# Attention with q's angles as pairs of 32-row products, v's sum taken from x's sum, and a new order on VectorE and GpSimd

## The chip, the cores and the metric

The kernel runs on one core of a Trainium2 chip. The metric is the device time of the whole launch in microseconds (us); smaller is better. The core has TensorE (PE: matmuls; PEld is its weight load), VectorE (DVE), ScalarE (ACT), GpSimd (POOL) and SyncE (SP, which here only issues DMAs). TensorE, VectorE, ScalarE and GpSimd each take their instructions in the order in which they are written; they meet through semaphores.

## What is computed

A layer of attention and a layer of experts over 8 sequences of 512 tokens with 128 features. Cut to what matters here, the attention is:

```python
q = (x @ Wq.T + bq).reshape(B, 512, 16, 8)      # k and v alike; 16 heads of 8
def fourier(h):
    p = einsum('blhd,dm->blhm', h, proj_mat) / sqrt(8)     # 128 angles a head
    return concatenate([cos(p), sin(p)], -1) / sqrt(128)
kv  = einsum('blhm,blhd->bhmd', fourier(k), v)
out = einsum('blhm,bhmd->blhd', fourier(q), kv)
x   = layernorm(x + out.reshape(B, 512, 128) @ Wo.T + bo)
# then: router, top 2 of 8 experts, two matmuls an expert, a second layernorm
```

Sine and cosine of p are made from p in turns: p/(2 pi), less its nearest whole number, and then sin(2 pi r) and the square of sin(pi r), since cos(2 pi r) = 1 - 2 sin(pi r)^2.

## The kernel before

**Stages.** A start-up of some 14 us, the attention over 8 sequences (`sequences(body)`, called batches 0 to 7 here), each of 16 units of work, and then the experts: 71 tiles of 128 rows, of which the last batch's layernorm, router and ranks are carried along. The end sums and normalizes.

**A unit** is 1024 columns of angles on 128 partitions: units 0 to 7 are k's, units 8 to 15 are q's. In unit u TensorE issues, in this order, `angles` of u (two 128x512 products into one of three PSUM slots of `ang`), `reduce_turns` of u-1 (minus the identity times the rounded turns, added to the same slot), and then one product with finished features: `kv_product` in units 4 to 11, `out_product(b, hg, a)` from unit 13 on and in units 0 to 3 of the next batch. Around them stand the pieces of a batch that come once: `x_T`, `project` (units 6 and 7, for batch b+1), `rows_T` (unit 8), `logits` (unit 9), `kv_turn` and `ranks` (unit 12), `c_product` (unit 14), `v_product` (unit 15). `rows_T`, `logits` and `ranks` belong to batch b-1.

**Angles.** q and k are each split in two float32r parts, written to `parts_dram` and read back by DMA as `stk`, 128 rows for 4 heads: 4 combinations of parts times 8 dimensions times 4 heads. `proj_stk` holds the projection for these rows, zero outside a head's own 32 rows. Before the change these 32 rows are spread over all partitions (dimension outside, head inside), so that each of q's products runs over all 128 rows.

**VectorE** rounds a unit's turns (`round_turns`, L1073), squares its share of the units two behind (`square`, L1081), and takes values out of PSUM: `kvT_evac`, `kv_evac`, `c_evac`, `v_evac`, `x_evac`, `take_logits`, `largest`, `which`, `take_ranks`, `move_base`, `slot_numbers`. The tuples BEFORE_ROUND, AFTER_ROUND and AFTER_SQUARE say at which unit and where in it they stand.

**ScalarE** runs the two sines of a unit (L885, L886) when the unit is reduced.

**GpSimd** squares the units of `POOL_SQ` (L1450), and for batch b-1 normalizes (`deviation`, `normalize`, L1475), picks experts (`chosen`; L1600 writes `picks`, for which `ranks` waits), and sends the rows with 8 indirect DMAs (`send_rows`, L1619) in units 14 and 15; for batch b+1 it splits k and q (L360).

**kv.** `kv_product` sums the features times v; `kvT_evac` takes both halves to SBUF, `kv_turn` turns them with two matmuls and adds -2 times v's sum with four more (L626), `kv_evac` copies the result to `kv_pad`, for which the first `out_product` waits. `c_product` makes the constant that `out_evac` adds.

## Time and profile before

| | before |
|---|---|
| time, median of 3 runs | 527.19 us (527.05 to 529.71) |
| the profiled execution: time, span of its instructions | 527.94 us, 526.1 us |
| granted TensorE clock, mean of the span | 0.976 |
| busy: PE, PEld, DVE, ACT, POOL | 484.8, 289.3, 411.4, 371.3, 393.2 us |
| batches 1 to 6 of the attention, each | 41.0 us |
| batch 0, from its first angles to batch 1's | 39.0 us |
| DMA moved | 53.94 MB, mean 103 GB/s |

The span runs from the profile's first instruction to the end of its last, 1.8 us less than the device time of that execution. "Busy" is the time in which an engine has an instruction of its own under way; matmuls overlap, so the distance from one group's start to the next one's start says more of TensorE than the sum of durations. A number in square brackets in a row is idle time of the engine ahead of the instruction, with what ended it.

### The profile page before, as it was taken

The page shows a single profiled execution, that of the slowest core. Times are in us where ns is not written, and L with a number is a line of the kernel's source. Part 1 is how long each engine was busy: PE and PEld are TensorE (multiplying, and loading weights), DVE is VectorE, ACT ScalarE, POOL GpSimd, SP SyncE. Part 2 cuts the span into 40 slices and gives each one's busy share as a digit, 9 for nine tenths or more (in the row PEclk, how much of TensorE's full clock was granted, in tenths as well). Part 3 has the DMA queues.
Part 4 walks back from the last instruction along what each step waited for, and adds up shares of the span by engine and source line. Part 5 has one row for each costly group of instructions (what it writes and reads, how often), then busy time and mean ns, then how long its engine had stood idle before and what let it go on. Part 6 is the DMA issues. An engine that isn't in the chain of part 4 may idle for free.

```text
span 526.1 us, 12307 instructions
## 1 busy us (share of the span) xinstructions
PE 484.8 (92%) x3819; PEld 289.3 (55%) x3819; DVE 411.4 (78%) x897; ACT 371.3 (71%) x505; POOL 393.2 (75%) x463
## 2 busy tenths in 40 slices
PE   6699999999999999999999999878999999999813
PEld 3344344345345345345334444438999988999801
DVE  4878978979979888888888887567678976777554
ACT  3698797887898798788788786576555555565225
POOL 2374298888888889779779879985777787687645
PEclk9899999999999999999999999899999999999957
DMA  4563053144154143244233221032222333222184
GB/s 110 168 198 122 21 161 121 52 132 154 47 161 159 40 143 126 65 127 150 67 110 122 87 61 46 2 73 59 72 62 73 88 97 101 68 73 63 37 307 177
DMA packets 44596, 53.94 MB, mean 103 GB/s; under 512 B 8419, under 2 KB 25093, under 8 KB 44533
## 3 DMA queue, kind: packets, MB, share of 16 engines
q1 hardware_dynamic: 39728, 43.82, 28.1%
q0 software_dynamic: 4320, 8.95, 5.2%
q8 instruction: 33, 0.54, 0.4%
q10 hardware_dynamic: 484, 0.38, 0.2%
q14 instruction: 31, 0.25, 0.1%
HBM read 33.09 MB, written 20.04 MB: 101 GB/s over the span
## 4 chain that ended last, share of the span: by engine, by line
PE 67%; POOL 15%; DMA 4%; issue 4%; SPq 3%; DVE 3%; ACT 2%; DVEq 0%; POOLq 0%; ACTq 0%
PE misc L647 11%; PE ang L798 10%; PE ang L807 10%; PE ang L592 8%; PE misc L612 6%; PE ang L584 6%; POOL rows_s L1475 5%; PE ang L579 5%; POOL feats L1450 4%; PE misc L531 1%; POOL rstd L1468 1%; ACT feats L886 1%; PE misc L678 1%; PE misc L626 1%; PE misc L662 1%
## 5 line engine op out<-in xcount | busy, mean ns | idle before, releaser
L1073 DVE TENSOR_SCALAR turns<-ang 128x1024 f16<-128x1024 f32 x128 | 155.9, 1219 | 48.8 <-PE ang L584 29.7
L885 ACT ACTIVATE feats<-ang 128x1024 f32<-128x1024 f32 x128 | 131.3, 1026 | 63.1 <-PE ang L592 62.2
L1450 POOL TENSOR_TENSOR feats<-feats 128x1024 f32<-128x1024 f32 x56 | 107.8, 1925 | 58.8 <-ACT feats L886 58.4
L886 ACT ACTIVATE feats<-ang 128x1024 f32<-128x1024 f32 x128 | 131.1, 1024 | 0.0
L1081 DVE TENSOR_TENSOR feats<-feats 128x1024 f32<-128x1024 f32 x72 | 93.2, 1295 | 0.9 <-ACT feats L886 0.9
L1619 POOL DMA_INDIRECT routed_dram<-rows_s,slots x64 | 76.5, 1195 | 19.2 <-issue 18.2
L1649 POOL DMA_INDIRECT expert_dram<-feats x71 | 69.8, 983 | 25.8 <-DVE feats L1374 16.9
L592 PE MATMUL ang<-turns,negi 128*128 128x512 f16 x256 | 77.9, 386 | 4.0 <-DVE turns L1073 4.0
L798 PE MATMUL ang<-feats 128*128 128x128 f32 x568 | 76.5, 278 | 3.2 <-ACT feats L953 1.4
L953 ACT ACTIVATE feats<-experts 128x644 f32 x71 | 52.5, 739 | 34.9 <-DVE feats L1374 27.5
L807 PE MATMUL ang<-experts,feats 128*128 x568 | 75.6, 276 | 0.5 <-DVE feats L1334 0.5
L798 PEld LDWEIGHTS ang<-feats 128*128 128x128 f32 x568 | 68.9, 192 | 6.8 <-DVE feats L1326 3.7
L612 PE MATMUL misc<-feats,v_pad 128*32 128x256 f32 x1024 | 70.0, 393 | 2.4 <-POOL feats L1450 2.4
L807 PEld LDWEIGHTS ang<-experts,feats 128*128 128x128 f32 x568 | 69.1, 192 | 1.3 <-issue 1.3
L647 PE MATMUL misc<-feats,kv_pad 128*32 128x512 f32 x512 | 66.1, 602 | 0.0
L1334 DVE TENSOR_TENSOR feats<-ang,feats 128x512 f32<-128x512 f32 x71 | 48.9, 689 | 21.4 <-PE ang L798 21.2
L612 PEld LDWEIGHTS misc<-feats,v_pad 128*32 128x32 f32 x1024 | 27.2, 110 | 41.7 <-issue 27.5
L579 PE MATMUL ang<-proj_stk,stk 128*128 128x512 f32 x128 | 48.8, 464 | 1.2 <-DMA stk<-parts_dram 0.6
L584 PE MATMUL ang<-stk,proj_stk 128*128 128x512 f32 x128 | 49.1, 465 | 0.0
L970 ACT ACTIVATE feats<-feats 128x128 f32<-128x128 f32 x71 | 28.1, 396 | 17.7 <-DVE feats L1383 8.5
L592 PEld LDWEIGHTS ang<-turns,negi 128*128 128x128 f16 x256 | 14.9, 99 | 41.7 <-issue 28.8
L579 PEld LDWEIGHTS ang<-proj_stk,stk 128*128 128x128 f32 x128 | 20.0, 191 | 32.2 <-issue 30.9
(201 smaller groups left out, 570.1 us busy)
## 6 DMA issues: line engine op xcount, KB each, us to landing
stk<-parts_dram SPq DMA_DIRECT2D x126, 128.0 KB, 2.7
parts_dram<-parts SPq DMA_DIRECT2D x16, 512.0 KB, 3.3
feats<-routed_dram SPq DMA_DIRECT2D x72, 65.5 KB
experts<-ffn_W SPq DMA_DIRECT2D x16, 256.0 KB, 3.2
feats<-expert_dram SPq DMA_DIRECT2D x16, 256.0 KB, 4.8
out<-feats SPq DMA_DIRECT2D x8, 256.0 KB, 2.0
x_all<-attn_x SPq DMA_DIRECT2D x7, 256.0 KB, 4.5
expert_dram<-feats POOLq DMA_INDIRECT x71
```

The lines of the kernel that those rows point to most:

```text
L579: mm = pe.matmul(a[:, t * 512:(t + 1) * 512], stk[:, 0, hg, tok:tok + P], proj_stk[:, :, :].rearrange("p g m -> p (g m)"), start=True, sto ...
L584: mm = pe.matmul(a[:, t * 512:(t + 1) * 512], proj_stk[:, 2 * half + t, :], stk[:, 1, hg, :], start=True, stop=False, skip_group_check=True)
L592: mm = pe.matmul(ang[:, slot(ph, u), t * 512:(t + 1) * 512], negi[:, :], turns[:, u % 2, t * 512:(t + 1) * 512], start=False, stop=True, s ...
L612: mm = pe.matmul(misc[32 * g:32 * g + 32, 0, 0:2 * FEAT].rearrange("p (a m) -> p a m", a=2), v_pad[:, 2 * half + t, g, hg * PADH:(hg + 1) ...
L647: mm = pe.matmul(misc[32 * g:32 * g + 32, 1, :], kv_pad[:, a, g, hg * PADH:(hg + 1) * PADH], feats[:, 2 * hg + g // 2, a, (g % 2) * LEN:(g ...
L798: mm = pe.matmul(h_bank[r % 2][:, j * P:(j + 1) * P], w_now[:, r % W_RING, j * P:(j + 1) * P], xgT[:, r % 2, :], start=True, stop=True)
L807: mm = pe.matmul(y_bank[r % 2][:, 0:P], hidT[:, r % 2, j * P:(j + 1) * P], expert(x_e)[:, j * P:(j + 1) * P], start=(j == 0), stop=(j == H ...
L885: act.activation(f[:, 0, :], a, ACT.Sin, scale=TWO_PI)
L886: act.activation(f[:, 1, :], a, ACT.Sin, scale=TWO_PI / 2).then_inc(s["sines"], 1)
L1073: dve.tensor_scalar(turns[:, u % 2, :], ang[:, slot(ph, u), :], MAGIC, -MAGIC, ALU.add, ALU.add)\
L1081: dve.tensor_tensor(f, f, f, ALU.mult).then_inc(s["sq_v"], 1)
L1450: pool.tensor_tensor(f, f, f, ALU.mult).then_inc(s["sq_p"], 1)
```

## The change

- **q's angles.** The operand is ordered by head: in `parts_dram` and `stk` a head's 32 rows (2 parts of the projection, 2 parts of q, 8 dimensions) stand together. q's product of head g takes only rows 32g to 32g+31, and the two heads of a unit stand on different rows of the array and write different banks. k's products are as before. Both copies are now made by the write: four DMAs of 256 KB where one of 512 KB stood; a read is one DMA of 256 KB where two of 128 KB stood. The projection's setup has one DMA instead of four and one more step on VectorE.
- **The reduction** of units 8 to 14 is cut into 32-column pieces: 8 matmuls with 8 weight loads instead of 2 with 2.
- **v's sum.** `x_evac` also sums x over the tokens, `v_total` (unit 9) makes v's sum with one small product, and `kvT_evac` adds it (times -2) while it copies; the four matmuls of L626, the scaled identity, `c_product` and the copy to `kv_c` go, and `kv_turn` is two transposes. `c_evac` now sums kvT itself, in two instructions.
- **Order on VectorE.** In unit 11 the square of unit 9 no longer stands behind `kvT_evac`; it stands in unit 12, behind `kv_evac`, `take_ranks` and `move_base`, which all come ahead of it.
- **Order on GpSimd.** It also squares unit 14, in unit 0 of the next batch, and of its 8 indirect DMAs two go out in each of units 14, 15, 0 and 1.

```diff
-POOL_SQ = (1, 3, 4, 6, 8, 10, 12)
+POOL_SQ = (1, 3, 4, 6, 8, 10, 12, 14)
...
                 hold(sp, "split", 2, b, side + 1)
-                dst = parts_dram[b, side].rearrange("i r n -> r i n")
-                sp.dma_start(dst, parts[:, side, :, :].bitcast(F32)).then_inc(s["parts_out"], 16)
-                hold(sp, "parts_out", 32, b, 16 * side + 16)
+                for j in range(PARTS):
+                    for i in range(PARTS):
+                        sp.dma_start(parts_dram[b, side, :, j, i], parts[:, side, i, :].bitcast(F32))\
+                            .then_inc(s["parts_out"], 16)
+                hold(sp, "parts_out", 32 * SPL, b, 16 * SPL * (side + 1))
...
                     for t in range(2):
-                        mm = pe.matmul(a[:, t * 512:(t + 1) * 512], proj_stk[:, 2 * half + t, :],
-                                       stk[:, 1, hg, :], start=True, stop=False, skip_group_check=True)
+                        g = 2 * half + t
+                        rows = slice(g * PADH, (g + 1) * PADH)
+                        mm = pe.matmul(a[:, t * 512:(t + 1) * 512], proj_stk[rows, g, :], stk[rows, 1, hg, :],
+                                       start=True, stop=False, skip_group_check=True)
...
+                tiles = [slice(32 * i, 32 * i + 32) for i in range(G)] if HALF <= u < UNITS - 1 else [slice(0, P)]
                 for t in range(2):
-                    mm = pe.matmul(ang[:, slot(ph, u), t * 512:(t + 1) * 512], negi[:, :],
-                                   turns[:, u % 2, t * 512:(t + 1) * 512], start=False, stop=True,
-                                   skip_group_check=True)
+                    for cols in tiles:
+                        mm = pe.matmul(ang[cols, slot(ph, u), t * 512:(t + 1) * 512], negi[:, cols],
+                                       turns[:, u % 2, t * 512:(t + 1) * 512], start=False, stop=True,
+                                       skip_group_check=True)
...
+            def v_total(b, *free):
+
+                wait(pe, *free)
+                pe.matmul(misc[:, 1, P:P + 2], wT[:, 2, :], x_sum[:, b % 2, :], start=True, stop=True,
+                          skip_group_check=True).then_inc(s["v_sum_mm"], 1)
...
                 wait(pe, "kvT_ev", 1, b, 1)
-                o = misc[:, 0, :]
-                pe.matmul(o[:, 0:P], kvT[:, 0, :], ident[:, :], start=True, stop=True, skip_group_check=True)
-                pe.matmul(o[:, P:2 * P], kvT[:, 1, :], ident4[:, :], start=True, stop=False, skip_group_check=True)
-                for t in range(LT):
-                    mm = pe.matmul(o[:, P:2 * P], minus_2[:, :], dense(v_pad[:, t, :, :]),
-                                   start=False, stop=(t == LT - 1), skip_group_check=True)
+                for a in range(2):
+                    mm = pe.transpose(misc[:, 0, a * P:(a + 1) * P], kvT[:, a, :], ident[:, :])
                 mm.then_inc(s["kv_mm"], 1)
...
             def kvT_evac(b):
                 wait(dve, "kvT_mm", HALF, b, HALF)
-                dve.tensor_copy(kvT[:, :, :].rearrange("p a m -> p (a m)"), misc[:, 0, 0:2 * P])\
-                    .then_inc(s["kvT_ev"], 1)
+                wait(dve, "v_sum_ok", 1, b, 1)
+                dve.tensor_scalar(kvT[:, 1, :], misc[:, 0, FEAT:2 * FEAT], 4.0, v_sum[:, :], ALU.mult, ALU.add)
+                dve.tensor_copy(kvT[:, 0, :], misc[:, 0, 0:FEAT]).then_inc(s["kvT_ev"], 1)
...
             def c_evac(b):
-                wait(dve, "c_mm", 1, b, 1)
+                wait(dve, "kvT_ev", 1, b, 1)
+                dve.tensor_reduce(c_raw[:, :], kvT[:, 1, :], AX.X, ALU.add).then_inc(s["c_raw_ok"], 1)
+                wait(dve, "c_raw_ok", 1, b, 1)
...
                     if u == 11:
                         kvT_evac(b)
+                    if u == 12:
+                        kv_evac(b)
...
-                    if not (first and u < 2):
+                    if not (first and u < 2) and u != 11:
                         square(b, u - 2)
+                    if u == 12:
+                        square(b, 9)
...
                     if u in (14, 15) and not first:
-                        send_rows(b - 1, u - 14)
+                        send_rows(b - 1, 0, range(2 * (u - 14), 2 * (u - 13)))
+                    if u in (0, 1) and b > 1:
+                        send_rows(b - 2, 1, range(2 * u, 2 * u + 2))
```

VectorE in units 11 to 14 of a batch, before (L1073 rounds a unit, L1081 squares one, L1085 is `kvT_evac`, L1147 `take_ranks`, L1092 and L1093 `kv_evac`, L1152 `move_base`, L1158 `slot_numbers`):

```order
L1073 TENSOR_SCALAR turns<-ang 128x1024
L1085 COPY kvT<-misc 128x256
L1081 TENSOR_TENSOR feats<-feats 128x1024
L1073 TENSOR_SCALAR turns<-ang 128x1024
L1147 TENSOR_TENSOR slot_m<-misc,base 128x32
L1092 COPY kv_c<-misc 128x128
L1093 COPY kv_pad<-misc 128x32x8
L1152 TENSOR_TENSOR base<-misc,base 128x8
L1073 TENSOR_SCALAR turns<-ang 128x1024
L1081 TENSOR_TENSOR feats<-feats 128x1024
L1158 TENSOR_REDUCE slots<-slot_k 128x8
L1073 TENSOR_SCALAR turns<-ang 128x1024
```

And in the changed kernel (L1079 rounds, L1087 squares, L1098 and L1099 are `kvT_evac`, L1105 `kv_evac`, L1161 `take_ranks`, L1166 `move_base`):

```order
L1079 TENSOR_SCALAR turns<-ang 128x1024
L1098 TENSOR_SCALAR kvT<-misc,v_sum 128x128
L1099 COPY kvT<-misc 128x128
L1079 TENSOR_SCALAR turns<-ang 128x1024
L1105 COPY kv_pad<-misc 128x32x8
L1161 TENSOR_TENSOR slot_m<-misc,base 128x32
L1166 TENSOR_TENSOR base<-misc,base 128x8
L1087 TENSOR_TENSOR feats<-feats 128x1024
L1079 TENSOR_SCALAR turns<-ang 128x1024
L1087 TENSOR_TENSOR feats<-feats 128x1024
L1172 TENSOR_REDUCE slots<-slot_k 128x8
L1079 TENSOR_SCALAR turns<-ang 128x1024
```

The first square, unit 9's, has moved from ahead of the rounding of unit 12 to behind all that unit 12 takes out of PSUM.

GpSimd from the picks of unit 11 to unit 3 of the next batch, before (L1600 writes `picks`, L1450 squares, L1611 is `slots_of_picks`, L1619 sends):

```order
L1600 TENSOR_TENSOR picks<-hot 128x32
L1602 TENSOR_TENSOR rows_s<-top 128x4
L1603 COPY rows_s<-pick_no 128x4
L1604 TENSOR_SCALAR rows_s<-rows_s 128x4
L1450 TENSOR_TENSOR feats<-feats 128x1024
L1611 TENSOR_TENSOR slot_k<-hot,slot_m 128x32 x2
L1450 TENSOR_TENSOR feats<-feats 128x1024
L1619 DMA routed_dram<-rows_s,slots 38016x131 x8
L1450 TENSOR_TENSOR feats<-feats 128x1024 x3
```

And in the changed kernel (L1620, L1468, L1631, L1639):

```order
L1620 TENSOR_TENSOR picks<-hot 128x32
L1622 TENSOR_TENSOR rows_s<-top 128x4
L1623 COPY rows_s<-pick_no 128x4
L1624 TENSOR_SCALAR rows_s<-rows_s 128x4
L1468 TENSOR_TENSOR feats<-feats 128x1024
L1631 TENSOR_TENSOR slot_k<-hot,slot_m 128x32 x2
L1468 TENSOR_TENSOR feats<-feats 128x1024
L1639 DMA routed_dram<-rows_s,slots 38016x131 x4
L1468 TENSOR_TENSOR feats<-feats 128x1024
L1639 DMA routed_dram<-rows_s,slots 38016x131 x4
L1468 TENSOR_TENSOR feats<-feats 128x1024 x3
```

The square of unit 14 now stands between the first and the second four of the eight sends; the rest of the row is as it was.

## Rows read from the trace of the kernel before

**Rows 1.** One steady stretch: start:end, us, each engine's busy time (instructions), granted clock, DMA

```profile
139.00:180.00 41.00, 40.74 (x320) 17.90 (x315) 35.34 (x57) 34.21 (x40) 34.69 (x33) 1.00 0.39 117
```

**Rows 2.** Waits of TensorE from 56 to 346 us: total us, times, longest

```profile
PE misc L671 <- POOL rows_s L1475: 1.8, 7, 0.3
```

**Rows 3.** The chain within 150 to 200 us, in order: start us, us, what

```profile
150.09 1.90 POOL feats L1450
...
157.34 0.66 PE misc L671 x4
...
161.92 1.00 PE misc L612 x16
```

**Rows 4.** Timeline of TensorE, four single matmuls of unit 10: start us, us

```profile
160.76 0.48 PE L584 MATMUL ang<-stk,proj_stk 128*128 128x512 f32 x1
...
161.08 0.40 PE L584 MATMUL ang<-stk,proj_stk 128*128 128x512 f32 x1
...
161.32 0.39 PE L592 MATMUL ang<-turns,negi 128*128 128x512 f16 x1
...
161.54 0.38 PE L592 MATMUL ang<-turns,negi 128*128 128x512 f16 x1
```

**Rows 5.** Timeline of TensorE, units 12 to 15 and unit 0's start

```profile
166.43 1.06 PE L626 MATMUL misc<-v_pad,minus 128*128 128x128 f32 x8
167.32 0.18 PE L688 MATMUL misc<-picks,tri 128*128 128x32 f16 x1
...
170.50 0.74 PE L584 MATMUL ang<-stk,proj_stk 128*128 128x512 f32 x2
...
173.29 0.60 PE L592 MATMUL ang<-turns,negi 128*128 128x512 f16 x2
...
175.74 0.70 PE L579 MATMUL ang<-proj_stk,stk 128*128 128x512 f32 x2
```

**Rows 6.** Timeline of VectorE in the same batch: squares (L1081) and a rounding (L1073)

```profile
159.65 1.82 DVE L1081 TENSOR_TENSOR feats<-feats 128x1024 f32<-128x1024 f32 x1
...
165.44 1.22 DVE L1081 TENSOR_TENSOR feats<-feats 128x1024 f32<-128x1024 f32 x1
...
169.55 1.21 DVE L1081 TENSOR_TENSOR feats<-feats 128x1024 f32<-128x1024 f32 x1
...
171.27 1.22 DVE L1073 TENSOR_SCALAR turns<-ang 128x1024 f16<-128x1024 f32 x1 [0.38 <-PE ang L584]
```

**Rows 7.** Timeline of GpSimd in the same batch, and its picks in the experts' stage

```profile
158.49 1.89 POOL L1450 TENSOR_TENSOR feats<-feats 128x1024 f32<-128x1024 f32 x1
160.34 2.26 POOL L360 TENSOR_TENSOR parts<-qk_f,parts 128x512 fp32r<-128x512 f32 x1
...
165.68 1.09 POOL L1600 TENSOR_TENSOR picks<-hot 128x32 f16<-128x32 f32 x1
...
167.24 1.89 POOL L1450 TENSOR_TENSOR feats<-feats 128x1024 f32<-128x1024 f32 x1
...
388.36 0.25 POOL L1600 TENSOR_TENSOR picks<-hot 128x32 f16<-128x32 f32 x1
```

**Rows 8.** Timeline of ScalarE: the two sines of unit 11

```profile
166.19 1.02 ACT L885 ACTIVATE feats<-ang 128x1024 f32<-128x1024 f32 x1 [0.17 <-PE ang L592]
167.11 1.02 ACT L886 ACTIVATE feats<-ang 128x1024 f32<-128x1024 f32 x1
```

**Rows 9.** Timeline of GpSimd at the attention's end: the fourth of the eight sends

```profile
349.58 1.52 POOL L1619 DMA_INDIRECT routed_dram<-rows_s,slots  x1 [0.30 <-issue]
```

**Rows 10.** Timeline of TensorE there: last four out_products, first layer of the first tile

```profile
350.63 1.92 PE L647 MATMUL misc<-feats,kv_pad 128*32 128x512 f32 x16
352.49 1.16 PE L798 MATMUL ang<-feats 128*128 128x128 f32 x8
```

**Rows 11.** Timeline of TensorE in batch 7: a wait and the group behind it

```profile
330.36 1.93 PE L612 MATMUL misc<-feats,v_pad 128*32 128x256 f32 x16 [2.38 <-POOL feats L1450]
```

**Rows 12.** Timeline of TensorE at the start, unit 2's angles

```profile
17.46 0.74 PE L579 MATMUL ang<-proj_stk,stk 128*128 128x512 f32 x2 [0.63 <-DMA stk<-parts_dram]
```

More of the change, by code:

```diff
@@ L384, in write @@
                 hold(sp, "split", 2, b, side + 1)
[L385 to L387 removed]
+                for j in range(PARTS):
[3 more added lines that the diff above has]
+                hold(sp, "parts_out", 32 * SPL, b, 16 * SPL * (side + 1))
             def read(b, side, hg):
                 hold(sp, "angles", UNITS, b, HALF * side + 2 * hg + 2 - UNITS)
[L393 to L397 removed]
+                rows = parts_dram[b, side].rearrange("(a g) j i d n -> a (g j i d) n", a=HG)
+                sp.dma_start(stk[:, side, hg, :].bitcast(F32), rows[hg]).then_inc(stk_in[side][hg], 16)
             def at_unit(b, u):
@@ L569, in angles @@
                 elif u == 0:
-                    wait(pe, stk_in[0][0], 16 * PARTS, b, 0)
+                    wait(pe, stk_in[0][0], 16, b, 0)
                 elif half == 0:
-                    wait(pe, stk_in[side][hg], 16 * PARTS, b, 16 * PARTS)
+                    wait(pe, stk_in[side][hg], 16, b, 16)
                 wait(pe, "sines", UNITS, b, u - RING + 1)
@@ L756, in body @@
                         rows_T(b - 1, *(("b2_ok", 1, 0, 2) if last else ("q_ev", 1, b, 2)))
-                    if u == 9 and not first:
-                        logits(b - 1, "xr_ev", 1, b, 0)
+                    if u == 9:
+                        v_total(b, *(("q_ev", 1, b, 2) if first else ("xr_ev", 1, b, 0)))
+                        if not first:
+                            logits(b - 1, "xr_ev", 1, b, 0)
                     if u == 12:
@@ L766, in body @@
                     if u == 14:
-                        c_product(b)
                         out_product(b, 1, 0)
@@ L868, in proj_evac @@
                 wait(act, "split", 2, b, side - 1)
-                wait(act, "parts_out", 32, b, 16 * side - 16)
+                wait(act, "parts_out", 32 * SPL, b, 16 * SPL * (side - 1))
                 act.activation(parts[:, side, 0, :], misc[:, bank, :], ACT.Identity,
@@ L913, in _ @@
             act.dma_start(negi[:, :], c_negi).then_inc(s["negi_in"], 16)
+            for g in range(G):
+                act.dma_start(bv_col[g * PADH:(g + 1) * PADH, :],
+                              bv.rearrange("(a g d) -> g a d", a=HG, g=G)[g].unsqueeze(2)).then_inc(s["bv_in"], 16)
             act.dma_start(b1_raw[:, :], b1.rearrange("e (j p) -> (e j) p", p=P)).then_inc(s["b1_in"], 16)
-            act.wait_ge(s["consts"], 1)
+            act.wait_ge(s["consts"], 2)
             act.activation(warm[:, :], zero_t[:, :], ACT.Sin)
@@ L1268, in _ @@
             LAST_ROUND = ((7, bias_add), (8, bias_add))
-            BEFORE_ROUND = ((6, moments), (10, take_logits), (13, move_base))
-            AFTER_ROUND = ((5, residual), (10, largest))
-            AFTER_SQUARE = ((5, statistics), (10, which), (12, take_ranks), (13, slot_numbers))
+            BEFORE_ROUND = ((6, moments), (10, take_logits))
+            AFTER_ROUND = ((5, residual), (10, largest), (12, take_ranks), (12, move_base))
+            AFTER_SQUARE = ((5, statistics), (10, which), (13, slot_numbers))
             def body(b, ph):
```

101 lines of the change are left out of this document (50 added, 51 removed).

## The prediction

> **What bounds the kernel now.** I read the windows first. In a steady stretch of 41 us TensorE has 40.74 us of work at the full granted clock; the others have 34 to 35 us [rows 1]. Six of the eight batches are such stretches. But the work is in a ring. TensorE's waits name GpSimd's normalize seven times, 0.3 us at the longest [rows 2], and the chain of waits goes through GpSimd from the square of unit 4 (150.09) over normalize to `rows_T` at 157.34 [rows 3], 7.25 us of GpSimd's own work that TensorE's units 5 to 7 just cover. The second such place is `picks`: GpSimd writes them from 165.68 to 166.77 [rows 7], and `ranks` starts at 167.32 [rows 5], 0.5 us behind. What TensorE saves ahead of `ranks` beyond that is waited away, unless picks come sooner.
>
> **One rule of the two engines, from rows.** VectorE's square of 159.65 takes 1.82 us where others take 1.21 [rows 6]; GpSimd's square of 158.49 is under way until 160.4 [rows 7]. 159.65 + 1.82 - 1.21 = 160.26: it began 1.77 us behind the start of GpSimd's square. GpSimd's split of 160.34 then takes 2.26 us and begins in effect when VectorE's square is over. And the picks take 1.09 us beside the square of 165.44, but 0.25 us in the experts' stage, where there is none [rows 6, 7]. So: VectorE's square and GpSimd's tensor_tensor exclude each other, and whoever comes second waits for the whole instruction. The Trainium skill says the same (SBUF — State Buffer, the section on the shared port: an exclusive lock, held for the whole instruction, also for a tensor_tensor with both inputs in SBUF); by that rule, the trace agrees, and the collisions below follow from the new order.
>
> **The parts on TensorE.** Single starts: 160.76, 161.08, 161.32, 161.54 [rows 4]. A float32r product of 512 columns takes 0.24 us, a float16 one 0.22, and the first of the angles 0.32, of which some 0.10 is its weights' load. The 16 matmuls of `kv_product` stand four side by side: 4 x 0.22 = 0.87 us; in the chain they take 1.00 [rows 3], so 0.13 goes to the change between 128-wide and 32-wide work (0.10) and a load. A bare unit is 0.10 + 0.10 + 0.48 + 0.44 + 0.13 + 0.87 = 2.12 us.
> - Two products on 32 rows each: if they run side by side, as the 32-column ones do, the angles cost 0.24 instead of 0.48; if not, 0.48 (nothing gained). No row shows row pieces; I take 0.24, since the column pieces do run together.
> - The reduction in 32-column pieces: two rounds of 0.22 as before, and the change of shape now stands ahead of it rather than behind it. A bare unit: 2.12 - 0.24 = 1.88. Where whole-array work is a neighbour (units 8, 9, 10, 12, 13), seven more changes a batch come in at 0.10: 0.7 us.
> - `kv_turn`: L626 is 167.32 - 166.43 = 0.89 us [rows 5], gone; the two transposes instead of four passes save 0.2; `c_product` 0.1; `v_total` adds 0.2.
> - Sum a batch: 8 x 0.24 - 0.7 + 0.89 + 0.2 + 0.1 - 0.2 = 2.2 us (0.3 without the side-by-side). If TensorE alone bounded: 8 x 2.2 = 17.6 us.
> The Trainium skill says (TensorEngine Tiling (Array Packing), Key Properties) that a change of tiling mode drains the engine, and the trace agrees with 0.10 for it. The Trainium skill also gives, in TensorE: Matmul & The Clock Gate (Part 3), 3.07x for four row tiles, which no row here shows; by it the 0.24 stands.
>
> **What becomes of it: one batch, step by step**, in times of the trace before, with the same start of the chain (GpSimd's square of unit 4 at 150.09).
> 1. To `rows_T` nothing changes. From there TensorE saves some 0.2 us up to unit 11 and 1.1 in unit 12, so it is at `ranks` at about 166.0 instead of 167.3.
> 2. Picks: unit 9's square is no longer beside them, so they take 0.25: ready at 165.93 instead of 166.77. Both arrive together. Unit 13's angles start at 166.2 instead of 167.5: 1.3 us gained.
> 3. GpSimd goes on to its square of unit 10 at 166.40 (167.24 before [rows 7]). VectorE comes to unit 9's square at 166.9, since `take_ranks` must follow `ranks` (picks + 0.7 at the earliest), and GpSimd's square follows the picks by 0.47. So VectorE always comes second: 166.40 + 1.77 = 168.17, done 169.3.
> 4. TensorE does angles (166.2 + 0.45), reduction (to 167.2) and out_product(0, 0) (to 168.1) and then waits 1.25 us for unit 9's square. It ends unit 13 at 170.2; before 170.5 [rows 5]. Of the 1.3 us 0.3 is left.
> 5. VectorE rounds unit 13 until 170.43 and wants unit 11's square. GpSimd, behind its slots (169.24 + 0.45), starts unit 12's square at 169.69; the sines it needs end at 169.5 (two sines, 0.92 apart, take 1.84 us a unit [rows 8], and unit 12's follow unit 11's at 167.64). So the square waits until 169.69 + 1.77 = 171.46, before 169.55 [rows 6]. The rounding of unit 14, which stands behind it, runs 172.7 to 173.94; before it began at 171.27 and even waited for TensorE [rows 6].
> 6. TensorE wants to reduce unit 14 at 172.6, gets to at 174.0 (173.29 before [rows 5]), and with 0.46 + 0.87 + 0.1 + 0.92 begins the next batch at 176.35; before 175.74 [rows 5]. 0.6 us lost.
> 7. In units 0 to 5 VectorE has one square less, worth 0.14 us of a wait in unit 4. GpSimd's square 14 and later sends end near 187.4, ahead of the use of unit 1's square. Its later start of unit 4's square is 0.47 us, which closes the ring: a batch is 41.0 + 0.47 = 41.5 us.
>
> **The other terms.** Batch 0 has no ranks but both collisions: +0.35 (-2 without them). Batches 1 to 6: 6 x 0.47 = 2.8. Batch 7: its GpSimd carries the tables of the experts, which bind at the same times as before: 0. At its end GpSimd's fourth send ends at 351.1 [rows 9]; then comes unit 14's square, 1.89 us, until 353.0, and the last out_product, which before started at 351.55 (350.63 + 0.92) and let the first tile start at 352.49 [rows 10], waits for it: +1.5. The start: unit 2's angles waited for the read of `stk` at 17.46 [rows 12]; the write is now four DMAs and twice the bytes, 1 to 2 us later, of which 1 is hidden behind VectorE's setup; Wv's load comes about 0.6 sooner: 0, between -0.6 and +1. In the steady batches reads come ten units ahead of use; nothing. Sum: 527.94 + 0.35 + 2.8 + 1.5 = 532.6 for the profiled execution; the median lies 0.75 below that execution, so 531.8, taken as 532.0. A difference under 0.5% is about what cannot be told from none.
>
> **Rivals.**
> - *Only the first collision* (20%). Point 5 hangs on 0.74 us: if unit 12's sines come behind 170.43, VectorE goes first, its square is done at 171.6, unit 14 is reduced at 173.0, and the batch is 40.5: 6 x -0.5 - 0.5 + 1.5 = -2.0, 525.2. Slower products on TensorE (no side-by-side: 0.9 us later at `ranks`) lead there.
> - *TensorE's gain is kept* (30%). For it: 2.2 us a batch are really taken out, GpSimd has 6 us without work in 41 [rows 1] and loses two waits, and squares may meet more kindly than in my walk. Against: steps 3 to 6. With some 1.7 us in each of seven batches and +1.5 at the end: 527.2 - 10.4 = 517; all of it, 2.2 x 7, gives 513.
> - *The clock falls in the new waits* (7%). After the wait of 2.38 us in batch 7 the next group takes 1.93 us instead of the usual 1.07 [rows 11], at 1.2 GHz. If the waits of steps 4 and 6 bring that once a batch, at about 1.7 us: 532 + 6 x 1.7 = 542, slower. It decides only if two waits of 1.3 us, 3 us apart, count like one long one.
> - *Both collisions* as forecast (43%), 529.5 to 534.5.
>
> **How the numbers follow.** Time 532.0. Faster by over 0.5% (below 524.6): the kept gain 0.30 and a third of the first rival, 0.07: 0.37. Within 0.5%: the rest of the first rival and the forecast's lower edge: 0.19. Slower: 0.44. The range of 8 in 10 goes from 515 to 537 and leaves out the full 2.2 us and the clock's fall; the forecast's own range is 529.5 to 534.5.
>
> **What would show it.** Steady batches 41.5 us apart; picks of 0.25 us; VectorE's square in unit 12 some 2.4 us long; idle TensorE of over 1 us ahead of the second out_product of unit 13 (released by a VectorE square) and ahead of unit 14's reduction (released by the rounding); bare q units of 1.88 us; the last out_product of batch 7 released by GpSimd's square. It is wrong if batches are 39 us apart, if the angles' pair starts 0.24 us or more apart, or if those waits are not there.

## The result, and the profile after

| | before | after |
|---|---|---|
| time, median of 4 runs each | 528.12 us (527.05 to 529.71) | 532.97 us (531.88 to 534.42) |
| the profiled execution: time, span | 527.94, 526.1 us | 531.88, 530.1 us |
| batch 1 begins (first angles) | 52.8 us | 52.2 us |
| a steady batch (2 to 6) | 41.00 us | 41.42 us |
| batch 7 begins | 298.7 us | 300.7 us |
| first layer of the first tile begins | 352.49 us | 356.22 us |
| from there to the end | 173.6 us | 173.8 us |

The ratio is 1.0091 (95% interval 1.0063 to 1.0120): the change makes the kernel 0.9% slower. TensorE has less work, and the kernel does not get shorter. The ratios of the experiments below leave out runs over 1.5% above the fastest of their own kernel: three of the ten of e3 (544.9 to 551.7 us) and two of the six of e7 (541.2 and 548.0 us), none of any other.

One steady batch of the changed kernel (the columns are those of [rows 1]):

```profile
134.90:176.38 41.48, 39.02 (x351) 15.90 (x349) 37.88 (x59) 33.95 (x39) 37.30 (x35) 1.00 0.49 141
```

TensorE had 40.74 us of work in 41.00 [rows 1] and now has 39.02 in 41.48; VectorE went from 35.34 to 37.88 us and GpSimd from 34.69 to 37.30. GpSimd has one square of 1.89 us more; VectorE has one of 1.21 us less and a few small steps more. The rest is time in which the two hold each other up, and it counts as busy. TensorE's waits from 56 to 300 us, which before were one line of GpSimd's [rows 2], are now:

```profile
PE ang L594 <- DVE turns L1079: 7.1, 6, 1.2
PE misc L645 <- DVE feats L1087: 6.5, 6, 1.1
PE misc L669 <- POOL rows_s L1493: 1.1, 6, 0.2
```

Two waits in each batch, 1.1 us for a square (L1087) and 1.2 us for a rounding (L1079). Here they are in the timeline of TensorE, batch 3, units 12 to 15:

```profile
166.12 0.19 PE L686 MATMUL misc<-picks,tri 128*128 128x32 f16 x1
...
167.40 1.07 PE L645 MATMUL misc<-feats,kv_pad 128*32 128x512 f32 x8
169.54 1.06 PE L645 MATMUL misc<-feats,kv_pad 128*32 128x512 f32 x8 [1.08 <-DVE feats L1087]
...
174.06 0.62 PE L594 MATMUL ang<-turns,negi 128*32 128x512 f16 x8 [1.19 <-DVE turns L1079]
...
176.38 0.71 PE L577 MATMUL ang<-proj_stk,stk 128*128 128x512 f32 x2
```

VectorE at the same place (L1087 squares units 9 and 11, L1079 rounds units 13 and 14):

```profile
167.17 2.32 DVE L1087 TENSOR_TENSOR feats<-feats 128x1024 f32<-128x1024 f32 x1
169.41 1.21 DVE L1079 TENSOR_SCALAR turns<-ang 128x1024 f16<-128x1024 f32 x1
170.55 2.20 DVE L1087 TENSOR_TENSOR feats<-feats 128x1024 f32<-128x1024 f32 x1
...
172.79 1.21 DVE L1079 TENSOR_SCALAR turns<-ang 128x1024 f16<-128x1024 f32 x1
```

And GpSimd (picks, squares of units 10 and 12, the first send):

```profile
165.81 0.25 POOL L1620 TENSOR_TENSOR picks<-hot 128x32 f16<-128x32 f32 x1
...
166.52 1.89 POOL L1468 TENSOR_TENSOR feats<-feats 128x1024 f32<-128x1024 f32 x1
168.37 1.44 POOL L1631 TENSOR_TENSOR slot_k<-hot,slot_m 128x32 f32<-128x32 f32 x2
169.77 1.89 POOL L1468 TENSOR_TENSOR feats<-feats 128x1024 f32<-128x1024 f32 x1
173.16 1.13 POOL L1639 DMA_INDIRECT routed_dram<-rows_s,slots  x1 [1.50 <-DVE slots L1172]
```

Both of VectorE's squares begin while one of GpSimd's is under way, 0.65 and 0.78 us behind its start, and they take 1.1 and 1.0 us longer than the 1.21 of [rows 6]. Each ends 1.08 us behind the end of GpSimd's, whenever it began. VectorE has three more such squares in a steady batch of the changed kernel (of units 15, 2 and 7: 1.42, 2.63 and 1.85 us), and the kernel before has two (1.47 and 1.82 us); TensorE waits for none of these. The roundings, which read PSUM, are not held: 1.19 to 1.23 us beside GpSimd's squares, in all profiles.

At the hand-over to the experts, GpSimd's fourth send, its square of unit 14, and TensorE's last out_product and the first tile (compare [rows 9] and [rows 10]):

```profile
351.26 1.89 POOL L1639 DMA_INDIRECT routed_dram<-rows_s,slots  x1 [0.30 <-issue]
353.18 1.90 POOL L1468 TENSOR_TENSOR feats<-feats 128x1024 f32<-128x1024 f32 x1
```

```profile
355.23 1.06 PE L645 MATMUL misc<-feats,kv_pad 128*32 128x512 f32 x8 [2.19 <-POOL feats L1468]
356.22 1.16 PE L797 MATMUL ang<-feats 128*128 128x128 f32 x8
```

### The profile page after: what moved, and what is told of

The parts are those of the page before. It is cut to its first block, busy times and chain, and to the rows that moved or that the text cites. A ratio compares the mean times of both kernels' runs of the same rounds, so it can differ in the third digit from the quotient of the medians.

```text
span 530.1 us, 12861 instructions
## 1 busy us (share of the span) xinstructions
PE 469.9 (89%) x4075; PEld 272.1 (51%) x4075; DVE 430.1 (81%) x914; ACT 368.8 (70%) x505; POOL 411.0 (78%) x471
## 4 chain that ended last, share of the span: by engine, by line
PE 46%; POOL 22%; DVE 15%; issue 9%; DMA 4%; SPq 3%; ACT 2%; ACTq 0%; DVEq 0%; POOLq 0%
PE ang L797 10%; PE ang L806 10%; POOL feats L1468 7%; DVE turns L1079 6%; PE misc L645 6%; POOL rows_s L1493 5%; PE ang L577 5%; PE ang L594 5%; DVE feats L1087 5%; PE misc L614 3%; POOL routed_dram L1639 2%; POOL rstd L1486 1%; PE misc L529 1%; PE misc L660 1%; ACT feats L885 1%
## 5 line engine op out<-in xcount | busy, mean ns | idle before, releaser
L1079 DVE TENSOR_SCALAR turns<-ang 128x1024 f16<-128x1024 f32 x128 | 155.6, 1217 | 36.6 <-PE ang L577 19.2
L1468 POOL TENSOR_TENSOR feats<-feats 128x1024 f32<-128x1024 f32 x64 | 126.4, 1975 | 38.9 <-ACT feats L885 37.3
L1087 DVE TENSOR_TENSOR feats<-feats 128x1024 f32<-128x1024 f32 x64 | 107.3, 1677 | 2.3 <-ACT feats L885 2.3
L1639 POOL DMA_INDIRECT routed_dram<-rows_s,slots x64 | 75.1, 1173 | 26.0 <-issue 15.9
L594 PE MATMUL ang<-turns,negi 128*32 128x512 f16 (+1 forms) x592 | 79.6, 390 | 11.2 <-DVE turns L1079 11.2
L645 PE MATMUL misc<-feats,kv_pad 128*32 128x512 f32 x512 | 68.6, 610 | 10.5 <-DVE feats L1087 8.3
L614 PE MATMUL misc<-feats,v_pad 128*32 128x256 f32 x1024 | 68.4, 387 | 2.2 <-POOL feats L1468 2.2
L614 PEld LDWEIGHTS misc<-feats,v_pad 128*32 128x32 f32 x1024 | 28.6, 110 | 36.8 <-issue 20.5
L594 PEld LDWEIGHTS ang<-turns,negi 128*32 128x32 f16 (+1 forms) x592 | 15.1, 95 | 47.2 <-DVE turns L1079 26.5
L1392 DVE SCALAR_TENSOR_TENSOR feats<-ang,feats 128x128 f32<-128x128 f32 x71 | 24.8, 349 | 10.8 <-PE ang L806 10.3
```

Of the source, the lines that this page charges most:

```text
L594: mm = pe.matmul(ang[cols, slot(ph, u), t * 512:(t + 1) * 512], negi[:, cols], turns[:, u % 2, t * 512:(t + 1) * 512], start=False, stop=True,
L614: mm = pe.matmul(misc[32 * g:32 * g + 32, 0, 0:2 * FEAT].rearrange("p (a m) -> p a m", a=2), v_pad[:, 2 * half + t, g, hg * PADH:(hg + 1) ...
L645: mm = pe.matmul(misc[32 * g:32 * g + 32, 1, :], kv_pad[:, a, g, hg * PADH:(hg + 1) * PADH], feats[:, 2 * hg + g // 2, a, (g % 2) * LEN:(g ...
L1079: dve.tensor_scalar(turns[:, u % 2, :], ang[:, slot(ph, u), :], MAGIC, -MAGIC, ALU.add, ALU.add)\
L1087: dve.tensor_tensor(f, f, f, ALU.mult).then_inc(s["sq_v"], 1)
L1468: pool.tensor_tensor(f, f, f, ALU.mult).then_inc(s["sq_p"], 1)
```

## The experiments

They ran on three other chips of the same kind (e1 to e4, e5 to e8, e9 to e12), on which the kernel before takes 542.7 to 543.7 us (medians of 23 to 29 runs). The steady batches repeat there unit by unit to 0.03 us; the experts' stage takes 12 to 15 us more. So each is compared with the kernel before on its own chip, and the mechanism is read from the lengths of the units: from the start of one unit's angles to the next one's, in a steady batch (2 to 6; the middle one of the five). In the table u9 is unit 9 and so on, and "bare" is a unit without any piece that comes once a batch (10 and 11). Unit 12 has `kv_turn` and `ranks`, unit 13 the first two out_products, unit 15 `v_product`.

```
                                u9    bare   u12   u13   u15   batch  ratio to before (95%)
before                         3.01   2.11   2.56  2.97  3.01  41.00  1
after (e5 repeats it)          3.05   1.84   1.62  4.14  4.01  41.42  1.0043 (1.0025-1.0060)
e1 square 9 early              3.05   1.84   2.32  3.31  2.75  41.17  1.0008 (0.9983-1.0034)
e2 square 14 on VectorE        3.05   1.84   1.62  4.14  4.01  41.54  1.0034 (1.0013-1.0055)
e3 both                        3.05   1.84   2.32  3.31  2.75  40.13  0.9888 (0.9852-0.9923)
e4 whole rows and reductions   3.23   2.11   1.44  3.79  4.46  42.10  1.0100 (1.0053-1.0147)
e6 before, with the new order  3.01   2.11   2.56  3.18  3.02  41.22  0.9972 (0.9948-0.9997)
e7 e3 and early writes         3.05   1.84   2.32  3.31  2.75  40.15  0.9864 (0.9813-0.9915)
e8 e3, whole reductions        3.18   1.97   2.27  3.31  2.88  40.75  one run
e9 e3, whole rows, reductions  3.23   2.11   1.44  4.16  3.02  41.20  1.0015 (0.9985-1.0045)
e10 square 11 late             3.05   1.84   1.62  4.14  3.41  40.85  0.9953 (0.9933-0.9973)
e11 e10, square 14, writes     3.05   1.84   1.62  4.14  3.41  40.94  0.9976 (0.9950-1.0002)
```

Theory A is the prediction's: VectorE's squares of units 9 and 11 come second behind GpSimd's of units 10 and 12, and that eats TensorE's gain. Theory B: GpSimd, with eight squares, is full.

**e1: square 9 early.**

```diff
-                    if not (first and u < 2) and u != 11:
+                    if not (first and u < 2):
                         square(b, u - 2)
-                    if u == 12:
-                        square(b, 9)
```

> The changed kernel, with unit 9's square back in unit 11, behind kvT_evac; all else as changed. Theory A (the two collisions of VectorE's squares 9 and 11 with GpSimd's squares 10 and 12 eat TensorE's gain): the picks take about 1.1 us again, but unit 13 no longer waits for a square, and VectorE is free for the square of unit 11 before GpSimd starts unit 12's; a steady batch falls from 41.42 to about 40.0 us (39.7 to 40.3), the whole to 522 us (520 to 525). Theory B (GpSimd, which now has eight squares, is full: in the changed kernel it works from 178.79 to 193.50 without a gap, and has 37.3 us of work and 2 us between its DMA issues in 41.4 us, so that the ring runs through it): the batch stays within 0.4 us of 41.42, the whole at 529 to 533.

Both waits of units 13 and 15 go, and batch 1 takes 39.97 us (41.34 in e5), as Theory A has it. But batches 2 to 6 take 41.17, outside the 39.7 to 40.3 expected: unit 2's reduction now waits 0.86 us. The timelines of VectorE, GpSimd and TensorE there:

```profile
177.50 2.54 DVE L1087 TENSOR_TENSOR feats<-feats 128x1024 f32<-128x1024 f32 x1
```

```profile
177.04 1.90 POOL L1466 TENSOR_TENSOR feats<-feats 128x1024 f32<-128x1024 f32 x1
```

```profile
181.84 0.61 PE L594 MATMUL ang<-turns,negi 128*128 128x512 f16 x2 [0.86 <-DVE turns L1079]
```

GpSimd's square of unit 14, sent ahead of VectorE's of unit 15 by 0.46 us, is a third collision. In batch 1 it isn't there: no sends stand before it (they begin with batch 1's own, in its unit 14). So the eighth square does cost, but by the moment at which it runs, not because GpSimd is full; Theory B has the number and not the mechanism.

**e2: square 14 on VectorE** (POOL_SQ without 14).

> The changed kernel, with unit 14's square back on VectorE. Theory A: the batch is set by the collisions of units 12 to 14, which stay; a steady batch stays at 41.4 us (41.2 to 41.6), and only the hand-over gains: the last out_product of batch 7 no longer waits for GpSimd (2.19 us of wait go), so the whole is 530 us (529 to 531). Theory B: GpSimd loses 1.89 us a batch; batches fall by over 1 us, the whole to 523 or less.

Batches of 41.54 us, as Theory A said, and B falls. The hand-over's wait for GpSimd is gone; what the last out_product then waits for is 0.28 and 0.72 us of data for the experts' transposes ahead of it. Alone, the edit gains nothing that shows clearly against e5.

**e3: both.**

> The changed kernel with both edits: unit 9's square in unit 11, unit 14's square on VectorE. Theory A: the gain of e1 and the hand-over's of e2 add up: 520 us (517 to 523), faster than the kernel before (528) too. Theory B: GpSimd relieved and the order restored, about 520 too; if B alone is right, e3 is as e2.

40.13 us a batch, 1.1% faster than the kernel before, and 1.3 us a batch under the changed kernel. Its ten runs spread more than those of the kernel before on this chip (534.9 to 551.7 us against 541.5 to 546.6); over all ten the median is 1.1% lower and the mean 0.6%. TensorE's waits from 51 to 293 us:

```profile
PE misc L686 <- POOL picks L1618: 3.7, 6, 0.6
PE ang L594 <- DVE turns L1079: 1.4, 6, 0.2
PE misc L669 <- POOL rows_s L1491: 1.1, 6, 0.2
```

The ring is back at `picks`, 0.6 us a batch, because square 9 stands beside them again, and the three waits of a batch sum to 1.0 us. The picks:

```profile
164.11 0.95 POOL L1618 TENSOR_TENSOR picks<-hot 128x32 f16<-128x32 f32 x1
```

**e4: whole rows and reductions** in the changed kernel.

```diff
-mm = pe.matmul(..., proj_stk[rows, g, :], stk[rows, 1, hg, :],
+mm = pe.matmul(..., proj_stk[:, g, :], stk[:, 1, hg, :],
...
-tiles = [slice(32 * i, 32 * i + 32) for i in range(G)] if HALF <= u < UNITS - 1 else [slice(0, P)]
+tiles = [slice(0, P)]
```

> The changed kernel, with q's products over all 128 rows of the array and the reduction of units 8 to 14 in whole products, as before; the operand order and all else as changed. TensorE then has 8 x 0.24 = 1.9 us a batch more of products and 0.7 less of changes of shape. Theory A: TensorE's time is waited away in units 13 and 14 anyway, but GpSimd's square of unit 12 comes later with its sines and VectorE's behind it; a batch is 41.4 to 42.1 us, the whole 532 to 537 us. Rival C (TensorE's gain does carry over into the time): 1.2 us a batch more, 541 us.

42.10, the upper end of Theory A. TensorE comes later to unit 13, the first collision shrinks (VectorE's square of unit 9 takes 1.64 us), the second grows (2.81 us), and the wait ahead of unit 14's reduction is 1.3 us. TensorE's 0.27 us a unit, 2.2 us a batch, are worth 0.68 us a batch while the collisions stand.

**e5: the changed kernel again**, on the chip of e6 to e8.

> The changed kernel itself, on the chip of the other runs of this group, to be set beside them. Its attention should repeat: steady batches of 41.42 us, batch 1 to start at 52.2 us, the last out_product of batch 7 waiting 2.2 us for GpSimd's square of unit 14. Its ratio to the kernel before was 1.009; the same here, 1.005 to 1.013, if the difference lies in the attention alone.

The steady batches repeat. Batch 1 begins at 53.6 us and not at 52.2, and the ratio is 1.0043, just under the range expected. Both are taken up with e12.

**e6: the kernel before with VectorE's new order only.**

```diff
-BEFORE_ROUND = ((6, moments), (10, take_logits), (13, move_base))
-AFTER_ROUND = ((5, residual), (10, largest))
-AFTER_SQUARE = ((5, statistics), (10, which), (12, take_ranks), (13, slot_numbers))
+BEFORE_ROUND = ((6, moments), (10, take_logits))
+AFTER_ROUND = ((5, residual), (10, largest), (12, take_ranks), (12, move_base))
+AFTER_SQUARE = ((5, statistics), (10, which), (13, slot_numbers))
...
+                    if u == 12:
+                        kv_evac(b)
...
-                    if not (first and u < 2):
+                    if not (first and u < 2) and u != 11:
                         square(b, u - 2)
+                    if u == 12:
+                        square(b, 9)
...
-                    if u == 12:
-                        kv_evac(b)
```

> The kernel before, with only VectorE's new order of units 11 to 13 (unit 9's square in unit 12, behind take_ranks, kv_evac and move_base); operand, reduction, v's sum, GpSimd's squares and sends as before. Theory A (the order brings the collisions): TensorE is at ranks at 167.3, so VectorE comes to unit 9's square at about 168.3 to 168.7, behind GpSimd's square of unit 10, which now starts at 166.4; the second out_product of unit 13 waits some 0.5 us, unit 11's square comes second behind GpSimd's square of unit 12, and unit 14's reduction waits over 1 us; steady batches of 41.7 to 42.3 us, the whole 1.0 to 1.8% slower than the kernel before. Rival D (the order costs only where TensorE has become faster): 40.8 to 41.2 us a batch, the same time as before.

41.22: below Theory A's range and at the upper end of its rival's. The order alone costs 0.22 us a batch, and the times show how near it is. VectorE, squares of units 9 and 11:

```profile
166.34 1.29 DVE L1081 TENSOR_TENSOR feats<-feats 128x1024 f32<-128x1024 f32 x1
...
168.69 1.21 DVE L1081 TENSOR_TENSOR feats<-feats 128x1024 f32<-128x1024 f32 x1
```

GpSimd, squares of units 10 and 12 and the slots between:

```profile
164.37 1.89 POOL L1452 TENSOR_TENSOR feats<-feats 128x1024 f32<-128x1024 f32 x1
166.30 1.44 POOL L1613 TENSOR_TENSOR slot_k<-hot,slot_m 128x32 f32<-128x32 f32 x2
168.72 2.94 POOL L1452 TENSOR_TENSOR feats<-feats 128x1024 f32<-128x1024 f32 x1 [0.97 <-ACT feats L886]
```

VectorE's square of unit 9 comes just as GpSimd's of unit 10 ends, and its square of unit 11 comes 0.03 us ahead of GpSimd's, which then takes 2.94 us, at nobody's cost. The same order that loses a lock twice in the changed kernel loses it hardly once here, since TensorE reaches `ranks` 1.3 us later.

**e7: e3 with early writes.** For batch 0 the high parts are written when ScalarE has made them, ahead of VectorE's split.

```diff
+                if first:
+                    sp.wait_ge(s["kq"[side] + "_ev"], 1)
...
+                for i in range(PARTS):
+                    if first and i:
+                        sp.wait_ge(s["split"], side + 1)
+                    for j in range(PARTS):
```

> The changed kernel with unit 9's square back in unit 11 and unit 14's square on VectorE, and at the start, for batch 0, the two writes of the high parts of k and q issued as soon as ScalarE has made them, ahead of VectorE's split, and those of the low parts behind it. Steady batches of 40.13 us. If unit 2's angles wait for the four issues of the write in a row (2.49 us, from 10.59), the wait of 3.5 us ahead of them falls by 1.2 us and batch 1 starts at 50.3 us instead of 51.5; if they wait for the transfers of twice the bytes, it stays within 0.3 us of 51.5. The whole: 1.1 to 1.5% faster than the kernel before.

Unit 2's angles wait 2.68 us instead of 3.56 for `stk`, and batch 1 starts at 50.4 instead of 51.5. So when the write is issued matters; that the four issues in a row are the cause is not shown. They still take 2.50 us (2.49 in e3) and only begin 0.75 us sooner, at 10.15, and the read is issued 5.35 us behind that, as in e3. In the kernel before one issue of 0.39 us stands there and the read follows 2.8 us behind it.

The batches are those of e3. The ratio is 1.4% under the kernel before; the six runs lie between 531.7 and 548.0 us, and their median is 0.7% under. So e3 and e7 can't be told apart. Its profiled execution shows one thing that may spread them: VectorE and ScalarE stand still in batch 6 with a releaser that the profile calls "remote" (the trace names no instruction for it), and the batch takes 44.75 us. On VectorE:

```profile
258.80 1.22 DVE L1085 TENSOR_SCALAR turns<-ang 128x1024 f16<-128x1024 f32 x1 [1.37 <-remote]
```

**e8: e3 with whole reductions.**

> The changed kernel with unit 9's square in unit 11 and unit 14's on VectorE, and the reduction of units 8 to 14 in whole products instead of 32-column pieces. By the prediction's price of a change of shape, 0.10 us, a bare q unit gets one more change ahead of the reduction or none less behind it: 1.93 to 2.04 us instead of 1.83, and a whole batch 40.1 to 40.9 us (part of it hides in the 0.6 us of wait for the picks). If changes of shape cost nothing on their own, 1.83 and 40.13 stay.

Bare units of 1.97 instead of 1.84: the 32-column pieces save 0.13 a unit, and the batch costs 0.62 more, as expected. The row pieces give the other 0.14 (2.11 to 1.97).

**e9: e3 with whole rows and whole reductions**; what is left is v's sum and the place of `kv_evac`.

> The changed kernel with unit 9's square in unit 11, unit 14's on VectorE, and q's products over all 128 rows with whole reductions: what is left of the change is v's sum, the new place of kv_evac and the operand's order. Without the collisions the old rule holds that TensorE's gain ahead of the picks counts until the picks bound: of the 0.9 us saved in unit 12 some 0.5 come through, a batch is 40.3 to 40.9 us, and the row pieces are worth only 0.2 to 0.7 us a batch beyond it, against 2.2 us of TensorE's time (8 units, 2.11 to 1.83). If instead TensorE's time counts in full, it is 40.13 + 2.2 = 42.3 us. The whole 0.3 to 1% faster than the kernel before in the first case, 1.5% slower in the second.

41.20, 0.2 above the kernel before and outside the 40.3 to 40.9 expected: v's sum, with `kv_evac` in its new place, brings nothing by itself. Unit 12 falls from 2.56 to 1.44 and unit 13 rises from 2.97 to 4.16. TensorE is through with `ranks` and now waits for VectorE's rounding of unit 12, which stands behind `kvT_evac` and square 9:

```profile
168.97 0.60 PE L594 MATMUL ang<-turns,negi 128*128 128x512 f16 x2 [0.88 <-DVE turns L1079]
```

```profile
166.54 1.23 DVE L1087 TENSOR_TENSOR feats<-feats 128x1024 f32<-128x1024 f32 x1
167.70 1.21 DVE L1079 TENSOR_SCALAR turns<-ang 128x1024 f16<-128x1024 f32 x1
```

The 0.89 us of L626 [rows 5] had been lying beside just this work of VectorE's. Beside square 9 GpSimd's instruction behind the picks is held up here, small as it is:

```profile
166.65 1.19 POOL L1620 TENSOR_TENSOR rows_s<-top 128x4 f32<-128x4 f32 x1
```

**e10: square 11 late.** The changed kernel with unit 11's square behind unit 14's rounding and `c_evac`.

```diff
-                    if not (first and u < 2) and u != 11:
+                    if not (first and u < 2) and u not in (11, 13):
...
+                    if u == 14:
+                        square(b, 11)
```

> The changed kernel with one edit: unit 11's square no longer stands behind the rounding of unit 13 but behind that of unit 14 (and c_evac); unit 9's square stays in unit 12, GpSimd's squares and sends stay. Theory A, step 5 (unit 11's square comes second behind GpSimd's of unit 12 and holds up the rounding of unit 14): the rounding of unit 14 starts at once, GpSimd gets its slots 2 us sooner, the wait of 0.62 us ahead of unit 14's reduction goes and a wait of some 0.7 us for unit 11's square comes ahead of the last out_product of unit 15; the first collision stays (1.06 us of wait in unit 13). A steady batch is 39.7 to 40.7 us instead of 41.42, the whole 520 to 527 us on the chip of the first runs, 0.5 to 1.3% faster than the kernel before. If the price lies in the first collision or elsewhere, it stays at 41.2 to 41.6 us.

The rounding of unit 14 starts at once, its reduction waits no more, and the batch falls by 0.57 us to 40.85, less than the 0.7 to 1.7 us expected. 0.46 us come back as a wait for the moved square:

```profile
172.53 1.06 PE L645 MATMUL misc<-feats,kv_pad 128*32 128x512 f32 x8 [0.46 <-DVE feats L1087]
```

**e11: e10 with square 14 on VectorE and the early writes.**

> The same edit, with unit 14's square on VectorE and the early write of the high parts for batch 0. Theory A: steady batches of 39.6 to 40.3 us, no third collision in units 1 to 3, no wait for GpSimd in the last out_product of batch 7, batch 1 starts at 50.4 us: 1.4 to 2.2% faster than the kernel before. If GpSimd's chain of sends and squares 1, 3 and 4 sets the floor, the batch stays at 40.1 us or above.

A miss: 40.94, and nothing gained on e10; batch 1 begins at 51.4 us and not at 50.4. With square 11 late, GpSimd's square 14 does not collide (VectorE's of unit 15 takes 1.43 us in e10), so moving it away brings nothing, and one more square on VectorE costs 0.08 in unit 4. The number fits the other reading too, that GpSimd's chain sets a floor of 40.1 or above, but the rows do not: as in e10, TensorE waits for GpSimd only 0.2 us a batch and for VectorE's squares 1.5.

**e12: the kernel before**, on the chip of e9 to e11.

> The kernel before, on this chip: steady batches of 41.00 us and batch 1 from 52.8 us as on the first chip; the 15 us that it takes longer here are to be in the experts' stage, behind 352.5 us. If batch 1 starts at 50 to 51 us instead, the 2.5 us by which the old kernel with the new order began batch 1 sooner are the chip's, not the order's.

The steady batches are the same 41.00. Batch 1 begins at 50.5 us instead of 52.8. What differs in the profiles is the clock. Windows of the kernel before on the first chip and here; the column behind the five engines is the granted clock:

```profile
20.00:27.00 7.00, 5.94 (x32) 2.22 (x36) 5.76 (x9) 4.59 (x6) 5.77 (x10) 0.76 0.55 170
```

```profile
20.00:27.00 7.00, 6.32 (x56) 2.46 (x58) 6.31 (x9) 6.51 (x8) 5.67 (x12) 1.00 0.55 167
```

In its profile of the first chip the kernel before had a stretch at 1.2 GHz in batch 0. The changed kernel had one on both chips, at or right behind the wait for `stk`, as had every kernel here with the new start (eleven profiles, waits of 2.4 to 3.6 us). On the first chip and in e5:

```profile
18.00:24.00 6.00, 5.37 (x22) 2.52 (x26) 4.61 (x7) 3.95 (x5) 1.93 (x2) 0.72 0.76 265
```

```profile
18.00:25.00 7.00, 5.95 (x14) 2.61 (x14) 4.58 (x8) 3.77 (x4) 1.79 (x1) 0.51 0.76 265
```

So the first chip's profiles hide what the changed kernel's start costs. Whether that lies in the chip or in the one execution is not shown. Batch 1 begins at 53.6 us in e5, at 50.5 in e12 and at 50.3 in e6, which has the old start and e5's chip: 3.1 to 3.3 us. In this run batch 7 of the kernel before had a stall of 3.8 us, and ScalarE's row shows the same releaser as in e7:

```profile
303.68 1.02 ACT L885 ACTIVATE feats<-ang 128x1024 f32<-128x1024 f32 x1 [4.06 <-remote]
```

e8, e9 and e11 had such a stall at that place too, of 6.3, 2.7 and 1.3 us, e1, e3 and e5 none. What it waits for, no row names. If it comes in most executions of the kernel before there, it would explain why most ratios on these chips lie about half a per cent under what the start and the batches say; one profile can't show that, and this part stays open.

## Why the prediction was right, step by step

Forecast was 532.0 us, with 529.5 to 534.5 for both collisions (43%) and 515 to 537 in all; measured was 532.97. The forecast lies 0.9% above the median that it started from, 527.19, and the measured time 0.9% above the kernel before.

The times of this section are those behind `rows_T` of the same batch, forecast and measured, so that the two kernels can be laid over each other (157.34 before [rows 3]; after, in the chain of waits, 157.47):

```profile
157.47 0.66 PE misc L669 x4
```

- **Steps 1 and 2.** TensorE at `ranks`: forecast some 8.7, measured 8.65 (9.98 before). Picks of 0.25 us, ready at 8.59, measured 8.59. Right.
- **Step 3.** GpSimd's square of unit 10 at 9.06, measured 9.05; VectorE comes to square 9 at 9.56, measured 9.70, and is done at 11.96, measured 12.02. Right: the rule read from two rows [rows 6, 7] carried to 0.1 us.
- **Step 4.** A wait of 1.25, measured 1.08; end of unit 13 at 12.9, measured 13.07.
- **Step 5.** GpSimd's square of unit 12 at 12.35, measured 12.30; VectorE's square 11 second, the rounding of unit 14 at 15.36, measured 15.32. Right.
- **Step 6.** Reduction of unit 14 at 16.66, measured 16.59; the next batch at 19.01, measured 18.91.
- **Step 7.** 0.14 us less in unit 4, measured 0.06 (3.29 to 3.23). The batch 41.47, measured 41.42. Not foreseen: VectorE's square of unit 2 collides too (2.63 us, the row below), but TensorE does not wait for it, and unit 7 pays 0.50 us for the change from `project` to row pieces, of which unit 8 gives 0.33 back (2.81 after 3.14).

```profile
187.15 2.63 DVE L1087 TENSOR_TENSOR feats<-feats 128x1024 f32<-128x1024 f32 x1
```

Batch 1 of e1 and the batches of e3 show that these collisions are the cause: without them 39.97 and 40.13 us. e6 shows that VectorE's new order is not enough to bring them, and e10 takes away the second alone. The exclusion of the two engines, which the Trainium skill states (SBUF — State Buffer, SBUF: two separate sides; a VectorE instruction with two SBUF inputs and a GpSimd one that reads SBUF: the first takes the port for its whole length), agrees with the rows: in batches 2 and 3 of the changed kernel ten squares of VectorE's begin 0.3 to 1.6 us behind the start of one of GpSimd's, and all end 1.08 or 1.09 us behind its end. It goes for small operands too: in e9 the 128x4 tensor_tensor takes 1.19 us beside a square.

**The other terms of the sum.** Batches 1 to 6: +2.8, measured +2.5 (248.5 against 246.0). Batch 7 and the hand-over: +1.5, measured 55.57 against 53.75, +1.8; the last out_product does wait for square 14, 2.19 us, and the fourth send took 1.89 us beside VectorE's square, 1.52 before. Start and batch 0: +0.35, measured -0.6. The experts' stage: nothing, measured +0.2. The sum is +4.0 us in span, forecast +4.7. That the start's term came so near is luck. The first angles come 1.7 us sooner than before (13.76) and the write is begun 0.7 us sooner (10.59 against 11.32), but the read is issued 1.8 us later (15.89 against 14.13), and so unit 2's angles wait 3.49 us where they waited 0.63 [rows 12] and come 1.2 us later; the forecast had 0 for both together:

```profile
12.07 1.17 PE L577 MATMUL ang<-proj_stk,stk 128*128 128x512 f32 x4 [0.56 <-ACT stk L925]
...
18.63 0.73 PE L577 MATMUL ang<-proj_stk,stk 128*128 128x512 f32 x2 [3.49 <-DMA stk<-parts_dram]
```

Where the old start keeps its clock (e6, e12, set against e5), the same term is +3.1 to +3.3 us. So it was mis-sized: TensorE also falls to 1.2 GHz behind the wait of 3.1 to 3.5 us, and in the first chip's profiles a stretch at 1.2 GHz on the other side hid it.

**TensorE's parts.** The sum of 2.2 us a batch was too high: TensorE's work fell by 1.7 us (40.74 to 39.02). A bare unit was forecast at 1.88 and is 1.84, but the split was wrong: side by side was to save 0.24 and the pieces of the reduction nothing. The two row products do start together, and the next group stands 0.43 us behind them (0.56 before):

```profile
162.94 0.50 PE L584 MATMUL ang<-stk,proj_stk 32*128 32x512 f32 x2
163.37 0.61 PE L594 MATMUL ang<-turns,negi 128*32 128x512 f16 x8
```

By e8, the row pieces save 0.14 and the column pieces 0.13, the latter presumably by sparing the changes of shape around `kv_product`; no row separates that.

**The rivals.** "TensorE's gain is kept" was priced at 1.7 us a batch, 517 us, without a walk. e3 is that case: no collision bears on TensorE, and the gain is 0.87 us a batch (41.00 to 40.13); the rows name what binds then, the picks (0.6 us) and, behind `kvT_evac` and square 9, the rounding of unit 12 (0.2 us). By e3's ratio its time would have been 521 (527.19 x 0.9888), so the range's lower end of 515 was too generous. "The clock falls in the new waits" did not happen in the changed kernel's steady batches, only behind the long wait of its start; in e3 it fell once in five steady batches, behind waits of 0.6 and 0.24 us that stand in every batch alike (and in e7 once too, 1.6 us):

```profile
126.00:128.00 2.00, 2.00 (x16) 0.46 (x8) 1.54 (x3) 1.40 (x2) 0.78 (x3) 0.50 0.60 194
```

It cost 1.44 us in e3. "Only the first collision" hung on 0.74 us; e10, where the second was taken away, gives 0.57 us a batch for it, and not the 1.0 of that rival, since the square is needed soon after.

## What to carry to other kernels

Where two engines exclude each other, lay their instructions over each other with times, not with busy shares: who comes second pays up to a whole instruction of the other, and a gain on a third engine can move it from one side of that line to the other (e6 and the changed kernel have the same order on VectorE, and its square of unit 11 begins 0.03 us ahead of GpSimd's in one and 0.78 us behind it in the other). A gain on the busiest engine is worth what the work beside it leaves open: v's sum took 1.1 us from unit 12 and gave nothing, row and column pieces took 2.2 and gave 1.07. Price the optimistic rival by the same walk as the forecast.

## What the runs showed that I had not expected

- 32-column pieces of a float16 product are no dearer than whole ones, and save 0.13 us a unit where 32-column work follows (e8 against e3).
- Two float32r products on 32 rows each start together, but the pair occupies 0.43 us until the next group, not 0.32.
- GpSimd's indirect DMAs, 0.96 us at the least, take up to 1.97 us where most of one of VectorE's squares lies beside them (sends of both kernels, and of e3). Some with 0.5 us of a square beside them still take 0.96.
- The same kernel takes 527 us on one chip and 542 to 544 on three others; the steady batches agree to 0.03 us a unit, and the difference lies in the experts' stage (173.6 and 186.3 us from the first tile to the end), where GpSimd stands idle ahead of the sends of the experts' results (L1649) for 36.7 us instead of 24.6, most of it for VectorE. The 71 tiles run alike, within some 2 us, from tile 0 to 21 and from 36 to 70; from 21 to 36 they take 30.1 and 30.2 us in the two profiles of the first chip and 40.0 to 42.5 in all twelve of the others. There VectorE stands still once for 4.0 to 4.8 us in eleven of the twelve, in neither of the first chip's, again for "remote". What that is, no row shows. In e12:

```profile
413.93 0.69 DVE L1334 TENSOR_TENSOR feats<-ang,feats 128x512 f32<-128x512 f32 x1 [4.09 <-remote]
```

- VectorE and ScalarE stand still, also for "remote", for up to 5.8 us at the start of batch 7 in four of the twelve profiles of the other chips, the kernel before included.
